# One Trainium2 kernel, one change: TensorE work recast into two tile shapes, transfers of a tile merged, and the loads of z moved two slots on

## The reference, cut to what matters

```
x: (8, 64, 96, 96) float32
x = x + conv_ref(ln_c(x))            # ln over the 64 channels
t = tokens of x                      # (8, 9216, 64)
t = t + ffn_ref(ln_t(t))
conv_ref: for shift s in (0, 2): roll x by (-s, -s); each half of 32 channels:
    q, k, v = qkv_w @ xh                         # 96 x 32
    attention in windows of 4 x 4 tokens, 8 heads of 4 channels, with a bias; + 3x3 depthwise conv of v
    roll back; the two shifts are added
ffn_ref: softmax(x @ router_w + router_b), best 2 of 8 experts, each a 64 x 64 matrix; weighted sum
```

## Time and profile before

| | |
|---|---|
| runs | 3475.89, 3484.97, 3493.27 us; median 3484.97 |
| the profiled execution | 3467.97 us, its span 3466.1 us |
| instructions in the span | 202400 |
| matmul records on PE | 84772, that is 883 for each of the 96 tiles |
| DMA packets | 447180, 517.72 MB, mean 149 GB/s |

### The profile page before, as it was taken

The page is one execution under the profiler, slowest core; times in us unless marked ns, Lnnn a source line. Parts: engine busy times, 40 slices in busy tenths (PEclk is TensorE's granted clock), DMA queues, the critical chain, the costliest instruction groups (busy, mean ns, idle before and its releaser), DMA issues.

```text
span 3466.1 us, 202400 instructions
## 1 busy us (share of the span) xinstructions
PE 3080.1 (89%) x84772; PEld 1797.6 (52%) x84772; DVE 2229.3 (64%) x4807; ACT 1620.3 (47%) x3362; POOL 2501.0 (72%) x4998
## 2 busy tenths in 40 slices
PE   4899998989989898988889989989889999999996
PEld 2555555555555455554555545555455555555552
DVE  2566666666666666676666667666666666666675
ACT  2554444444444454444445444444444445454541
POOL 4887767767777677777767777777677777777760
PEclk7999999999999899999999999999999999999997
DMA  2456565555656565565556555555555565656555
GB/s 63 109 136 168 145 160 140 160 145 149 160 140 165 140 160 147 146 160 139 159 150 156 153 153 154 155 149 149 149 149 158 150 162 152 168 152 165 156 147 156
DMA packets 447180, 517.72 MB, mean 149 GB/s; under 512 B 120976, under 2 KB 415376, under 8 KB 446096
## 3 DMA queue, kind: packets, MB, share of 16 engines
q1 hardware_dynamic: 280336, 390.69, 41.4%
q0 software_dynamic: 165888, 113.57, 13.2%
HBM read 312.67 MB, written 77.86 MB: 113 GB/s over the span
## 4 chain that ended last, share of the span: by engine, by line
PE 64%; SPq 10%; issue 9%; DMA 9%; DVE 4%; ACT 4%; DVEq 0%; ACTq 0%
PE bank L622 15%; PE bank L707 11%; PE bank L687 10%; PE bank L607 7%; DMA z<-fin 3%; SPq L501 3%; PE bank L713 3%; PE bank L647 3%; PE bank L727 3%; PE bank L660 3%; SPq L531 3%; DMA gate_rows<-gateT 2%; PE bank L721 2%; PE bank L732 2%; PE bank L746 2%
## 5 line engine op out<-in xcount | busy, mean ns | idle before, releaser
L575 POOL DMA_DIRECT2D vx<-vt x3072 | 1555.6, 515 | 458.1 <-PE bank L713 446.1
L563 POOL DMA_DIRECT2D kx<-k_sb x1536 | 737.1, 488 | 419.0 <-issue 268.7
L707 PEld LDWEIGHTS bank<-probT,vx 128*32 128x32 f32 x36864 | 607.9, 150 | 438.2 <-issue 393.9
L622 PE MATMUL bank<-kx,qx 32*32 32x64 f32 x36864 | 705.3, 226 | 107.3 <-issue 79.9
L622 PEld LDWEIGHTS bank<-kx,qx 32*32 32x32 f32 x36864 | 597.5, 111 | 387.8 <-issue 374.2
L707 PE MATMUL bank<-probT,vx 128*32 128x16 f32 x36864 | 672.2, 210 | 139.7 <-issue 126.8
L939 DVE TENSOR_TENSOR gx<-gate_wide,yn_pair 128x768 f32<-128x768 f32 x384 | 365.6, 953 | 463.3 <-DMA gate_wide<-gate_rows 293.6
L796 ACT ACTIVATE prob<-prob 128x512 f32<-128x512 f32 x576 | 360.3, 626 | 267.1 <-DVE prob L951 253.4
L687 PE MATMUL bank<-halo,conv_w 128*64 128x380 f32 (+6 forms) x2592 | 460.3, 482 | 1.1 <-issue 1.1
L951 DVE TENSOR_TENSOR prob<-bank,row_max 128x512 f32<-128x512 f32 x576 | 398.5, 692 | 16.7
L946 DVE TENSOR_REDUCE row_max<-bank 128x32 f32<-128x512 f32 x576 | 382.7, 664 | 38.1 <-PE bank L622 30.0
(11 more groups left out here) (72 smaller groups left out, 2969.7 us busy)
## 6 DMA issues: line engine op xcount, KB each, us to landing
gate_wide<-gate_rows SPq DMA_DIRECT2D x768, 192.0 KB
vx<-vt POOLq DMA_DIRECT2D x3072, 12.0 KB
halo<-xn SPq DMA_DIRECT2D x160, 240.0 KB
kx<-k_sb POOLq DMA_DIRECT2D x1536, 24.0 KB
z<-fin SPq DMA_DIRECT2D x192, 192.0 KB, 5.7
yn_pair<-yn POOLq DMA_DIRECT2D x384, 96.0 KB
xa<-in_x SPq DMA_DIRECT2D x192, 96.0 KB, 4.3
xn<-xa SPq DMA_DIRECT2D x192, 96.0 KB
```

What stands on the lines that cost most here:

```text
L563: pool.dma_start(kx[to + m:to + C:4, r % 2, m, :], k_sb[at + m:at + C:4, r % 2, :])\
L575: pool.dma_start(vx[to:to + TOK, r % 2, col:col + 13:4, odd, :], vt[at:at + TOK, r % 2, x::2, :, :].rearrange("p h n k -> p h (n k)"))\
L622: last = MM(bank_s[r % 2][at, w * KEYS:(w + 1) * KEYS], qx[at, kr % 2, win, :, :].rearrange("p a i -> p (a i)"), kx[at, kr % 2, :, win * T ...
L707: last = MM(bank_o[32 * c:32 * c + 32, at * TOK:(at + 1) * TOK], vx[:, kr % 2, :, at % 2, at // 2 * 4 + ba], probT[:, kr % 2, at, ba * TOK ...
```

## The change

- v is computed beside q and k, in the same [32x32] tile shape, into the bank of the softmax sums (`bank_d`); the stage `value` is gone, and PE does q, k, v right behind the scores. Heads and channels are renumbered for it in the tables, which the host lays out.
- All other matmuls that had 64 or 128 output columns are cut into 32-column pieces (`columns`), so that PE knows two shapes only, [32x32] and [128x32]; in a slot all of the first come before all of the second.
- The router is computed with the tokens on the partitions, so that its logits need no turn: `logits` and `logitT` are gone; DVE adds the bias while it copies, at the start of slot 0 rather than in slot 2. q, k, v of slot 0 wait for that copy (`logit_saved`).
- Pairs of transfers of 64 partitions become one of 128 (`halves`): x, xn, xt, the output, z0t, z2t. `load_tile` keeps xt alone; z is loaded by a new stage, `load_z`, two slots later. Rows of z lie in another order (`(m l)` for `(c l q)`), so that one transfer fetches them.
- gateT has 128 partitions, cleared once.

```
 LAG = dict(
-    centre=0, variance=1, store_xn=2, load_strips=9, value=11, query_key=12,
+    centre=0, variance=1, store_xn=2, load_strips=9, query_key=12,
...
-    store_z=24, load_halo=29, load_tile=33, conv=34, ... router=41, logits=44,
-    take_logits=44, gates=45, ...
+    store_z=24, load_halo=29, load_tile=33, load_z=35, conv=34, ... router=41,
+    take_logits=42, gates=45, ...
...
+        def columns(bank, cols, weights, moving, **flags):
+            for c in range(0, 128, 32):
+                last = MM(bank[c:c + 32, cols], weights[:, c:c + 32], moving, **flags)
+            return last
...
+            def halves(flat, im, t):
+                return flat[im][:, :, t * 2 * SPX:(t + 1) * 2 * SPX].rearrange("b c (f n) -> f (b c) n", f=2)
             def load_x(r, im):
-                for half in range(2):
-                    at = (r % IMT * (2 * SP) + half * SP) * W
-                    sp.dma_start(xa[half * C:(half + 1) * C, r % 2, :], ...
+                sp.dma_start(xa[:, r % 2, :], halves(x_flat, bass.ds(im, 1), r % IMT)).then_inc(x_loaded[r % 2], 16)
...
                 if ti := s.tile("load_tile"):
                     k, r = ti
+                    if s.later(r, 2):
+                        wait_alone(sp, y_made, k - 1)
+                    sp.dma_start(xt[:, r % 2, :], halves(xt_flat, bass.ds(s.image(r, IMT), 1), (r + 1) % IMT))\
+                        .then_inc(xt_loaded[r % 2], 16)
+                if ti := s.tile("load_z"):
+                    k, r = ti
...
                     for p in range(2):
                         wait_alone(sp, z_stored[p], counts[p] * 16)
-                    if s.later(r, 2):
-                        wait_alone(sp, y_made, k - 1)
...
-                    for half in range(2):
-                        put_x(half)
-                        put_z(z0t, half, 0, 0, 0, 4, 0, t * (2 * SP) + half * SP, SP)
-                    put_rolled(0, 0, (t * (2 * SP) + H - ROLL) % H, ROLL)
-                    put_rolled(0, ROLL, t * (2 * SP), SP - ROLL)
-                    put_rolled(1, 0, t * (2 * SP) + SP - ROLL, SP)
+                    sp.dma_start(z0t[:, r % 2, :], halves(z_of[0], im, t)).then_inc(z_loaded[r % 2], 16)
...
+                        sp.dma_start(z2t[:, r % 2, :], z_of[1][im][:, :, at:at + 2 * SPX].rearrange("b c (f n) -> f (b c) n", f=2))\
+                            .then_inc(z_loaded[r % 2], 16)
...
-                        last = MM(bank_f[half * C:(half + 1) * C, 0:SPX], const("experts")[:, p * C:(p + 1) * C], gx[:, p % 2, half, :],
-                                  start=False, stop=(p == PAIRS - 1), skip_group_check=True)
+                        for c in range(0, C, 32):
+                            last = MM(bank_f[half * C + c:half * C + c + 32, 0:SPX],
+                                      const("experts")[:, p * C + c:p * C + c + 32], gx[:, p % 2, half, :],
+                                      start=False, stop=(p == PAIRS - 1), skip_group_check=True)
...
-                if st := s.strip("value"):
...
-                    MM(bank_p[0][:, 0:SPX], wv, xs[:, r % 4, :], start=True, stop=True).then_inc(v_made, 1)
                 if st := s.strip("query_key"):
...
+                        pe.wait_ge(fln_made, ti[0] + 1)
                         pe.wait_ge(logit_saved, ti[0] + 1)
+                    if s.later(r, 4):
+                        pe.wait_ge(log_made, k - 3)
...
                     for g in range(4):
-                        at, to = slice(g * CH, g * CH + CH), slice((g + 2) % 4 * CH, (g + 2) % 4 * CH + CH)
+                        at, to_v, to_k = (slice((g + n) % 4 * CH, (g + n) % 4 * CH + CH) for n in range(3))
                         q_last = MM(bank_p[0][at, 0:SPX], wq[at, at], xs[at, r % 4, :], start=True, stop=True)
-                        k_last = MM(bank_p[1][to, 0:SPX], wk[at, at], xs[at, r % 4, :], start=True, stop=True)
+                        k_last = MM(bank_p[1][to_k, 0:SPX], wk[at, at], xs[at, r % 4, :], start=True, stop=True)
+                        v_last = MM(bank_d[to_v, 0:SPX], wv[at, at], xs[at, r % 4, :], start=True, stop=True)
...
-                    MM(bank_p[1][0:GE, 0:SPX], const("router"), yn[:, r % 2, :], start=True, stop=True)\
-                        .then_inc(logitT_made, 1)
+                    for blk in range(TBLK):
+                        for c in range(4):
+                            last = MM(bank_p[1][32 * c:32 * c + 32, blk * GE:(blk + 1) * GE],
+                                      yn[:, r % 2, blk * 128 + 32 * c:blk * 128 + 32 * c + 32], const("router"),
+                                      start=True, stop=True)
```

More of the change, by code:

```diff
@@ L664, in slot @@
-                expert(1)
-                if ti := s.tile("logits"):
-                    k, r = ti
-                    pe.wait_ge(ln_made, tiles_to(s, k + (LAG["logits"] - LAG["variance"]) // TSLOT + 1))
-                    wait_alone(pe, logitT_saved, k + 1)
-                    for blk in range(TBLK):
-                        last = nc.tensor.transpose(bank_p[1][:, blk * GE:(blk + 1) * GE],
-                                                   logitT[:, blk * 128:(blk + 1) * 128], const("ident", GE)[:, 0:GE])
-                    last.then_inc(logit_made, 1)
+                    columns(bank_p[1], slice(0, SPX), const("mean"), sq[:, r % 2, :], start=True, stop=True).then_inc(var_made, 1)
@@ L686, in slot @@
                             at = half * SP + skip
-                            last = MM(by_rows(bank_c[half * C:(half + 1) * C, 0:SPX])[:, top:end, low:high],
-                                      conv_w[:, which, group * 3 + side, :],
-                                      by_rows(halo[:, r % 2, :])[:, at + top:at + end, low + dw:high + dw],
-                                      start=first[half], stop=(side == 2 and group == 1), skip_group_check=True)
+                            for c in range(0, C, 32):
+                                last = MM(by_rows(bank_c[half * C + c:half * C + c + 32, 0:SPX])[:, top:end, low:high],
+                                          conv_w[:, which, group * 3 + side, c:c + 32],
+                                          by_rows(halo[:, r % 2, :])[:, at + top:at + end, low + dw:high + dw],
+                                          start=first[half], stop=(side == 2 and group == 1), skip_group_check=True)
                             first[half] = False
@@ L731, in slot @@
                     pe.wait_ge(q_saved, strips_to(s, 2 * k + 10) * 2)
-                    MM(bank_p[0][:, 0:SPX], const("mean"), ysq[:, :], start=True, stop=True).then_inc(fvar_made, 1)
+                    columns(bank_p[0], slice(0, SPX), const("mean"), ysq[:, :], start=True, stop=True).then_inc(fvar_made, 1)
                 if ti := s.tile("router"):
@@ L940, in gate_product @@
                         .then_inc(gx_made, 1)
+                if ti := s.tile("take_logits"):
+                    k, r = ti
+                    dve.wait_ge(logit_made, k + 1)
+                    V.tensor_tensor(logits[:, :], bank_p[1][:, 0:TBLK * GE], const("router_bias"), ALU.add)\
+                        .then_inc(logit_saved, 1)
                 shift = s.unit("shift")
```

168 lines of the change are left out of this document (77 added, 91 removed).

## The result

The changed kernel takes 4270.73 us (median of four runs, 4269.4 to 4271.3), the kernel before 3484.39 beside it: a ratio of 1.2256, 95% interval 1.2225 to 1.2287. The forecast was 3162, range 3050 to 3320: wrong in sign and far outside.

The account below looks back on a forecast made before the run. It took PE to bound slots 4, 5 and 0, and a PE, DVE and ACT path slots 1 to 3. Gains of 2.78 + 0.85 = 3.63 us per period, times 89, are 323: 3485 - 323 = 3162 us, range 3050 to 3320.

Parts of the forecast that it names:

- SP's new slack of 5.1 us and more: On SP's queue: its 5.1 us wait per tile for z's landing would be over, hiding the merged transfers at no cost.
- clock and stops as before: Whole period: assumed that time lost to half clock (2.1 us) and to instructions not coming would not change.
- The prices of groups: On PE: start-to-start times for each group of matmuls in its new tile shape, such as 0.65 us for four 32-column tiles.
- the rule on row tiles and one bank: The skill's rule that different row tiles cannot share a PSUM bank at once; weighed for q, k, v, rejected from a profile row (0.81).
- Slots 1 to 3: Part of the period bound by a path through PE, DVE and ACT: 14.93 us to 14.24, a gain of 0.69.
- the lateness: Gates reaching DVE and PE late through SP's queue; taken as gone, worth 0.85 us per period, bounds 0 and 1.7.
- Slots 4, 5 and 0: Part of the period where PE waits for nobody: 16.84 us to 14.75, a gain of 2.09.
- PE's 1.48 us before pair 2: One PE wait of 1.48 us in the timeline, before the second expert pair, cited as evidence that late gates cost time.
- Slower: the clock: Rival, chance 0.05: PE idles longer before tile_sum, the clock stays at half through slots 4 and 5; 3807 us.
- Row groups in turn: Rival, chance 0.04: the q, k, v matmuls run one row group after another, 2.6 us; 3322 us.
- a wait of q, k, v for the logits: Slot 0, a sign of being wrong: q, k, v held by DVE's logits copy, forecast half a microsecond ahead of PE.
- the 198 us of the clock: Whole span: at most 5.7%, 198 us, lost to stretches at 1.2 GHz; the prediction put it at 2.1 us per period.

Follow-up runs that it names:

- split kernel: The changed kernel with every merged transfer issued again as two of 64 partitions, the rest of the change kept: 3671.75 us, 1.0499 of the kernel before.

## Why the prediction was wrong, step by step

- **The step that failed first: "The merged stores and loads carry the same bytes; cost nothing, hidden behind SP's new slack of 5.1 us and more."** They cost 612 us. The bytes are the same and the width is not: two DMA engines of 16. Nor was the slack cover enough: SP's queue is in order, what stands at its front delays all behind it, and six merges used the slack up (SP's waits for xa: 989 us in the split kernel, 76 in the changed one). The sentence that without cover ten transfers less "could still only shorten the queue" was as wrong: SP issued fewer transfers and stood longer at some (5.9 us for one z2t in the median).
- **The step that failed second: "clock and stops as before".** With the merges undone the stops grew from 227 to 597 us. The clock took some 140 us more by the estimate above, and the two ate the 310 us that PE's groups would have given, and 200 more. The prediction had the stops before it ("stops in which instructions do not come", 3.11 us) and saw them as a price of the loop's return. That every block of instructions may bring one, and that tiles of a quarter of the width are four times the instructions for the same columns, it did not price; only the time on the array was.
- **The prices of groups held**: 0.65 for four tiles, 0.84 for q, k, v (forecast 0.81), the convolution 1.28 to 1.31 (1.32), the logits 0.31 (0.35), medians of steps at full clock in the split kernel's trace. The scores ahead of q, k, v missed, 1.16 for 0.92, and the experts' bias took 0.81 for 0.76. On q, k, v the row was right to speak against the rule on row tiles and one bank, 2.6 us by it.
- **Slots 1 to 3** went as forecast: from 16.90 us before to 16.25 in the split kernel, start to start of the scores, mean of 80 periods (gain 0.65, forecast 0.69 with the lateness apart). **Slots 4, 5 and 0**, the dense ones, went from 18.35 to 21.23 where 2.09 less was forecast; slot 0 alone, 6.39 before, took 8.91, stops and half clock included.
- **The lateness**: the size was near (1.1 us, taken 0.85) on the kernel before, but by luck as far as the path goes. The prediction took PE's 1.48 us before pair 2 for the rule; PE has 12 such waits in the whole run, 22.3 us. That the gain can vanish behind another limit was not seen.
- **The rivals.** None named the width of the transfers or the blocks of instructions. "Slower: the clock" had the sign and a part of the mechanism. The mean granted clock did fall, from 0.943 to 0.827, under the 0.9 that the prediction gave as a sign of being wrong, and to 0.903 in the split kernel, where its share is some 140 us beside 370 of stops. In the changed kernel PE has 2% of the chain, so by that chain its 1098 us of busy time at half clock do not set the time. "Row groups in turn" and a wait of q, k, v for the logits did not occur. A slip that changes nothing: the 198 us of the clock are 2.2 per period over 89, not 2.1.
- **Left open:** how much of the six merges' price comes by the two engines' load and how much by the order of SP's queue, once SP's slack is gone; what ties the stops to the density, and the clock to either; and why z2t merged alone gains 1.5%.

## What to carry to other kernels

Before two transfers are merged, look at the outermost dimension of the merged pattern: if it is the number of parts that were merged, the transfer runs as narrow as that, and a queue in order hands its slowness to everything behind it. Read a change of tile shapes in instructions as well as in columns: on an engine that already shows "issue" gaps, narrower tiles that shorten its steps also raise the density of its instructions, and here the gain was paid back as stops. A gain shown on one bound (z's loads, 100 us) must be tried on the kernel where that bound stands; on another it was worth nothing.

## What the runs showed that was not expected

A transfer of 128 partitions whose pattern has 2 outermost ran at 31 to 51 GB/s alone, one of two times 64 partitions at 167. SP's issue of z2t, 0.58 us at its quickest, took up to 7.6 us in the changed kernel, and never over 0.63 where it alone was merged. Where PE resumes 1 to 2 us after the end of a 16,384-byte packet of its instruction queue, the median is 1.4 us in every kernel here. 11,520 one-column records took 472.8 us of PE's busy time on a single column tile, 41 ns each, and 215.4 us, 19 ns each, on four tiles in turn.
